# Flow attention in a decoder kernel: token totals and inverses laid out as 128 rows by 128 columns, spread by row tiles in plain fp32 into a ring of five banks

## The reference, cut to what matters

```python
qkv = x @ qkv_w.T + qkv_b                       # q, k, v per head
q = jax.nn.sigmoid(q); k = jax.nn.sigmoid(k)
k_sum = k.sum(axis=2)
sink_incoming = 1.0 / jnp.sum((q + EPS) * (k_sum[:, :, None, :] + EPS), axis=-1)
q_sum = q.sum(axis=2)
source_outgoing = 1.0 / jnp.sum((k + EPS) * (q_sum[:, :, None, :] + EPS), axis=-1)
k_so_sum = (k * source_outgoing[..., None]).sum(axis=2, keepdims=True)
conserved_sink = jnp.sum((q + EPS) * (k_so_sum + EPS), axis=-1) + EPS
q_si_sum = (q * sink_incoming[..., None]).sum(axis=2, keepdims=True)
conserved_source = jnp.clip(jnp.sum((k + EPS) * (q_si_sum + EPS), axis=-1) + EPS, -1.0, 1.0)
sink_allocation = jax.nn.sigmoid(conserved_sink)
source_competition = jax.nn.softmax(conserved_source, axis=-1) * float(n)
kv = jnp.einsum('bhnd,bhnm->bhdm', k, v * source_competition[..., None])
out = jnp.einsum('bhnd,bhdm->bhnm', q * sink_incoming[..., None], kv) * sink_allocation[..., None]
out = out.transpose(0, 2, 1, 3).reshape(b, n, c) @ proj_w.T + proj_b
```

## Time and profile before

| what | value |
| --- | --- |
| device time, three runs | 2602.89, 2605.04, 2608.36 us (median 2605.04) |
| the profiled execution: its time | 2608.17 us |
| its span, first to last instruction | 2606.3 us |
| busy share of the span | PE 90%, PEld 50%, DVE 61%, ACT 48%, POOL 27% |
| mean granted TensorE clock | 0.979 of full speed |
| chain that ended last, by engine | PE 61%, DVE 18%, ACT 14%, issue 4%, POOL 2% |

### The profile page before, as it was taken

The page is one execution under the profiler, slowest core; times in us unless marked ns, Lnnn a source line. Parts: engine busy times, 40 slices in busy tenths (PEclk is TensorE's granted clock), DMA queues, the critical chain, the costliest instruction groups (busy, mean ns, idle before and its releaser), DMA issues.

```text
span 2606.3 us, 37060 instructions
## 1 busy us (share of the span) xinstructions
PE 2350.9 (90%) x13000; PEld 1303.8 (50%) x13000; DVE 1591.2 (61%) x3101; ACT 1247.5 (48%) x2870; POOL 691.7 (27%) x989
## 2 busy tenths in 40 slices
PE   7989999989988999998898999999899899999866
PEld 3655544545565544454556554435455655444443
DVE  4664643569866462457977655155797746516698
ACT  5763212259675321227967431222886723122396
POOL 0002140037401232013820213201480031310366
PEclk9999999999999999999999999999999999999988
DMA  8001010010210200001030101001003010100000
GB/s 300 18 11 49 24 45 33 0 49 1 87 50 10 72 29 17 32 1 49 9 128 2 55 26 29 32 17 49 1 9 128 2 58 23 29 17 1 0 1 33
DMA packets 58988, 99.43 MB, mean 38 GB/s; under 512 B 13364, under 2 KB 13748, under 8 KB 58296
## 3 DMA queue, kind: packets, MB, share of 16 engines
q1 hardware_dynamic: 58808, 97.06, 11.3%
HBM read 88.66 MB, written 8.39 MB: 37 GB/s over the span
## 4 chain that ended last, share of the span: by engine, by line
PE 61%; DVE 18%; ACT 14%; issue 4%; POOL 2%; DMA 0%; ACTq 0%; DVEq 0%; POOLq 0%; SPq 0%
PE psum L398 20%; PE psum L392 13%; ACT prob L810 6%; PE psum L424 4%; PE psum L483 3%; DVE neg_max L1106 3%; PE psum L549 2%; DVE f_a L1113 2%; PE psum L451 2%; PE psum L791 2%; DVE bn L1056 2%; DVE f_top L1392 2%; PE psum L620 1%; ACT f_z L1008 1%; PE psum L763 1%
## 5 line engine op out<-in xcount | busy, mean ns | idle before, releaser
L398 PE MATMUL psum<-weights,mixed 128*128 128x512 f32 x768 | 341.2, 595 | 0.0
L392 PE MATMUL psum<-xT,weights 128*128 128x512 f32 x768 | 334.5, 593 | 0.0
L810 ACT ACTIVATE prob<-psum,neg_max 128x128 f32<-128x128 f32 (+3 forms) x512 | 265.0, 543 | 109.3 <-DVE neg_max L1106 109.3
L1430 POOL TENSOR_SCALAR var<-stats 128x1 f32<-128x1 f32 x192 | 63.8, 332 | 797.2 <-DVE stats L1057 797.1
L1106 DVE TENSOR_REDUCE neg_max<-psum 128x1 f32<-128x128 f32 (+3 forms) x512 | 217.5, 483 | 81.2 <-PE psum L488 46.5
L846 ACT COPY xT<-psum 128x512 f32<-128x512 f32 x128 | 70.3, 590 | 367.4 <-PE psum L451 367.4
L1087 DVE TENSOR_TENSOR x<-psum,x 128x512 f32<-128x512 f32 x128 | 88.4, 691 | 244.8 <-PE psum L398 172.7
L398 PE MATMUL psum<-weights,xT 128*128 128x512 f32 x512 | 232.9, 598 | 2.4 <-DVE recip L1295 1.6
L1443 POOL TENSOR_TENSOR f_a<-f_a,f_z 128x256 f32<-128x256 f32 x256 | 204.5, 809 | 113.8 <-DVE f_a L1113 113.8
L392 PEld LDWEIGHTS psum<-xT,weights 128*128 128x128 f32 x768 | 144.0, 190 | 172.4 <-issue 172.2
L398 PEld LDWEIGHTS psum<-weights,mixed 128*128 128x128 f32 x768 | 141.6, 190 | 167.5 <-issue 166.7
(11 more groups left out here) (246 smaller groups left out, 4193.1 us busy)
## 6 DMA issues: line engine op xcount, KB each, us to landing
xT<-in_xT SPq DMA_DIRECT2D x8, 1024.0 KB, 6.4
x<-in_x SPq DMA_DIRECT2D x8, 1024.0 KB, 8.9
out<-x SPq DMA_DIRECT2D x16, 512.0 KB, 2.8
weights<-in_a_k SPq DMA_DIRECT2D x4, 1024.0 KB, 5.3
weights<-in_a_q SPq DMA_DIRECT2D x4, 1024.0 KB, 5.1
weights<-in_a_v SPq DMA_DIRECT2D x4, 1024.0 KB, 5.0
w1f<-in_w SPq DMA_DIRECT2D x4, 1024.0 KB, 14.9
w2f<-in_w SPq DMA_DIRECT2D x4, 1024.0 KB, 17.3
```

Of the source, the lines that this page charges most:

```text
L392: last = mm(bank[:, 0:n], weights[weight][:, c, heads(g)], rhs(c), start=(c == 0), stop=(c == C - 1))
L398: last = mm(bank, lhsT(c), weights[weight][:, c, :], start=(c == 0), stop=(stop and c == C - 1))
L810: last = run(sb["prob"][:, slot, o:o + keys], bank[:, o:o + keys], ACT.Exp, bias=sb["neg_max"][:, n, qc, j:j + 1], accum_out=sb["a_sum"][: ...
```

## The change

Stage D's per-token numbers are laid out otherwise. A window of 512 tokens is cut in four quarters of 128. Where one bank held 32 rows per chunk (each head's value in eight equal rows) by 512 tokens, it now holds for each head a row (pair) per quarter, by 128 tokens: `d_quarters` issues 16 matmuls of 128 columns, which accumulate over the quarters `c` with weights that are zero outside the quarter's rows (`quarters`). VectorE's add and reciprocal then work on 128 x 128. `d_spread` takes each chunk's 32 rows as a row tile of the array and issues 16 plain fp32 matmuls of 32 rows to 128 columns, 128 tokens wide, into four banks at once; ScalarE's and GpSimd's split into halves goes away, and so do `d_coarse`, `d_halves` and `d_sel_r`. `dve_ring` is widened by banks 6 and 7 from the first `d_sums` to the first `d_out`. `d_source` is one step for both windows (256 columns), `d_weigh` one transpose per window in place of four. The constants are split in four `d_sums` steps with a `d_weights` step of VectorE ahead of each, and the order of the list is new: the weights from q's sums, `d_sums` and `d_total 1` stand among the last projections of k, `d_spread 1` ahead of the last of them, and the sinks stand behind `d_weigh 1`.

```diff
+OF_K, OF_Q, OF_SOURCE, OF_SINK = range(4)
+SUM_ORDER = [OF_Q, OF_K, OF_SINK, OF_SOURCE]
+TOTAL_ORDER = [1, 3, 0, 2]
+    def widen(self, banks):
+        n = len(self.names)
+        k = (n - self.first) % len(self.banks)
+        self.banks, self.first = banks + self.banks[k:] + self.banks[:k], n
+    def narrow(self, pe, banks):
+        self.drained(pe)
+        self.banks = banks
...
+    steps += [("d_weights", OF_Q), ("d_project", 1, 1, 0), ("d_sums", OF_Q), ("d_total", 1), ("d_project", 1, 1, 1), ("d_project", 1, 1, 2),
+              ("d_spread", 1), ("d_project", 1, 1, 3), ("d_table",)]
...
+    steps += [("d_turn", 0), ("d_turn", 1), ("d_total", 3), ("d_weights", OF_K), ("d_value", 0), ("d_sums", OF_K), ("d_total", 0), ("d_spread", 3),
+              ("d_value", 1), ("d_total", 2), ("d_spread", 0), ("d_weights", OF_SINK), ("d_value", 2), ("d_turn", 2), ("d_spread", 2),
+              ("d_value", 3), ("d_sums", OF_SINK), ("d_weights", OF_SOURCE), ("d_value", 4), ("d_turn", 3),
+              ("d_sums", OF_SOURCE), ("d_source",), ("d_value", 5), ("d_turn", 4), ("d_turn", 5), ("d_value", 6), ("d_weigh", 0), ("d_turn", 6),
+              ("d_turn", 7), ("d_value", 7), ("d_weigh", 1)] + [("d_sink", 0, g) for g in range(C)] + [("d_kv",)]
...
-            def d_compact(bank, i, src, w):
-                for g in range(C):
-                    last = mm(bank[HD * g:HD * g + HD, :], sb["d_thin"][:, i, g, :], src[:, g, tokens(w)],
-                              start=True, stop=True)
-                last.then_inc(dve_ring.filled, 1)
+            def d_quarters(bank, i, src, w):
+                for c in range(WT):
+                    for g in range(C):
+                        last = mm(bank[HD * g:HD * g + HD, :], sb["d_thin"][:, i, c, g, :], src[:, g, w * D + P * c:w * D + P * c + P],
+                                  start=(c == 0), stop=(c == WT - 1))
+                return last
...
                 elif kind == "d_spread":
-                    pe.wait_ge(q["d_halves_ready"], at("d_halves_ready", n + 2))
-                    for g in range(C):
-                        mm(dve_ring.claim(pe, ("d_spread", n, g)), sb["d_sel_r"][:, g, :], sb["d_halves"][:, n % 2, :],
-                           start=True, stop=True).then_inc(dve_ring.filled, 1)
+                    pe.wait_ge(q["d_inverse_ready"], at("d_inverse_ready", TOTAL_ORDER.index(n) + 1))
+                    spread = [dve_ring.claim(pe, ("d_spread", n, g)) for g in range(C)]
+                    for c in range(WT):
+                        for g, bank in enumerate(spread):
+                            r = slice(HD * g, HD * g + HD)
+                            last = mm(bank[:, heads(c)], sb["d_sel"][r, c, :], sb["d_inv"][r, n, :], start=True, stop=True)
+                            if c == WT - 1:
+                                last.then_inc(dve_ring.filled, 1)
+                elif kind == "d_source":
                     bank = dve_ring.claim(pe, step)
+                    for w in range(W):
+                        last = d_quarters(bank[:, heads(w)], OF_SOURCE, sb["d_kT"], w)
...
-            def eps_weights(sums, out, blocks):
+            def eps_weights(i, sums, out, pattern):
+                of_chunk = sb["d_tot"][:, i, :]
+                link(v.scalar_tensor_tensor(of_chunk, sums[:, 0, :], FLOW_EPS, sums[:, 1, :], ALU.add, ALU.add))
+                each = of_chunk[:, :, None].broadcast_to([P, C, P]) if i == OF_SINK else \
+                    of_chunk[:, None, :, None].broadcast_to([P, WT, C, HD])
+                v.tensor_tensor(out, pattern, each, ALU.mult).then_inc(q["d_weights_ready"], 1)
```

More of the change, by code:

```diff
@@ L662, in _ @@
                     bank = dve_ring.claim(pe, step)
-                    for g in range(C):
-                        mm(bank[HD * g:HD * g + HD, 8:10], sb["d_thin"][:, 2, g, :], sb["flow_eps"][:], start=True, stop=True)
-                    for g in range(C):
-                        last = mm(bank[:, 2 * g:2 * g + 2], sb["d_blk"][:, C + g, :], sb["flow_eps"][:], start=True, stop=True)
+                    for w in range(W):
+                        last = d_quarters(bank[:, heads(w)], OF_SOURCE, sb["d_kT"], w)
@@ L667, in _ @@
                     last.then_inc(dve_ring.filled, 1)
-                elif kind == "d_source":
-                    d_compact(dve_ring.claim(pe, step), 2, sb["d_kT"], arg[0])
                 elif kind == "d_weigh":
                     w, = arg
-                    pe.wait_ge(q["d_e_ready"], at("d_e_ready", w + 1))
-                    bank = dve_ring.claim(pe, step)
-                    for t in range(WT):
-                        last = nc.tensor.transpose(bank[:, heads(t)], sb["d_inv"][:, W + w, heads(t)], ident[:])
-                    last.then_inc(dve_ring.filled, 1)
+                    pe.wait_ge(q["d_e_ready"], at("d_e_ready", 1))
@@ L678, in _ @@
+                    nc.tensor.transpose(dve_ring.claim(pe, step)[:, 0:P], sb["d_e"][:, heads(w)], ident[:]).then_inc(dve_ring.filled, 1)
                 elif kind == "d_kv":
                     taken(pe, ("d_turn", T - 1))
-                    bank = dve_ring.claim(pe, ("d_esum",))
-                    for g in range(C):
-                        last = mm(bank[:, 2 * g:2 * g + 2], sb["d_sel"][:, g, :], sb["d_esum"][:], start=True, stop=True)
-                    last.then_inc(dve_ring.filled, 1)
+                    pe.wait_ge(q["d_shares_ready"], at("d_shares_ready", 1))
@@ L706, in _ @@
                     w, t = divmod(arg[0], WT)
+                    if w + t == 0:
+                        dve_ring.narrow(pe, banks[3:6])
                     taken(pe, ("d_fold", C - 1))
@@ L1323, in _ @@
+                        v.tensor_tensor(vt, vt, e, ALU.mult).then_inc(dve_ring.freed if t == WT - 1 else q["d_v_weighed"], 1)
                 elif kind == "d_kv":
-                    bank = dve_ring.take(dve, ("d_esum",))[:, 0:2 * C].rearrange("p (g w) -> p g w", w=W)
-                    v.tensor_reduce(sb["d_fac"][:], bank, AX.X, ALU.add).then_inc(dve_ring.freed, 1)
+                    bank = dve_ring.take(dve, ("d_esum",))
+                    v.reciprocal(sb["d_fac"][:], bank[:, 0:C]).then_inc(dve_ring.freed, 1)
@@ L1624, in place @@
     put("blocks", [P])
-    put("odd_rows", [1])
+    put("quarters", [WT, HD])
     put("stacked", [SK])
```

174 lines of the change are left out of this document (80 added, 94 removed).

## The result

The changed kernel takes 2559.97 us (median of 4 runs, 2558.67 to 2560.47) against 2606.35 us for the kernel before (4 runs, 2602.89 to 2608.36): a ratio of 0.9823, 95% interval 0.9806 to 0.984, 46.4 us less on the medians. The profiled execution took 2559.72 us with a span of 2557.9, where before it was 2608.17 and 2606.3: 48.4 us less.

What follows compares the result with a forecast made beforehand. TensorE, busy 90% of the span, was taken as the bound; 46.0 us content plus 0.5 us waits per entry gave 52.7 us less, 2555.5 us, and 3.1 us to the median made 2552 us, range 2539 to 2576.

Steps and rivals of the forecast that it cites:

- TensorE's content: Stage D's steps to the first `d_kv` matmul, added up by kind without waits: 46.0 us per batch entry.
- the halves of the source: Two halves of `d_source` in stage D, each priced like a total from stage A's records: 1.01 us each.
- `d_weigh` with the sum of exponentials: Stage D: two transposes for `d_weigh`, 0.3 us, and one 128-column load with a narrow matmul, 0.3 us.
- Waits: TensorE's waits in stage D, mostly covered by VectorE, narrowly at three places: 0.5 us per entry in all.
- The loads: A spread's 32 weight loads in stage D: about 1.1 us, still fitting; bounds for the whole 2545 and 2566 us.
- the stage A row: Stage A's 16 loads of 32 x 128 within 0.54 us, 0.03 each, taken to decide the spreads' load time.
- the series rival: Row tiles' loads pass one after another: 3.9 us a spread in stage D, 2597 us in all; chance 0.08.
- The gain: Stretch from last k projection to `d_kv`: 14.2 us less in the first entry, 12.8 in each other, 52.7 total.
- I let it stay up: Clock in stage D's stretch: no fall, since no stand is near the 1.44 us after which it fell.
- From the profile to the median: Whole kernel: the median of the runs lies 3.1 us below the profiled execution, so 2555.5 becomes 2552 us.
- The slower rival: Each spread record in stage D waits for its own load: 7.4 us a spread, 2653 us; chance 0.03.
- the hidden-gain rival: Work behind `d_kv` waits on something of its own, so an earlier start is lost; chance 0.02 with no change.

Runs made afterwards that it cites:

- the banks and the turns' order alone: Kernel before with a five-bank ring in stage D and turns 0 to 3 ahead of the first constants: 2584.28 us, ratio 0.9915.
- the seams: Changed kernel with turns moved to make six more borders between tiled and full-size groups: 2552.70 us, one execution only.
- the two filled gates: Changed kernel with stage C's third base tile ahead of the first gate, 2538.81 us; then also the sixth ahead of the fifth output tile, 2539.15 us.
- the first filled gate: Changed kernel with only stage C's third base tile moved ahead of the first gate: 2538.81 us, ratio 0.9749 to the kernel before.
- the banks alone: Kernel before with the ring of five banks in stage D and nothing else of the change: 2594.27 us, ratio 0.9949.

## Why the prediction was right, and where it was off

The forecast was 2552 us, 2539 to 2576. The mechanism held; three sizes were off: the stretches by 1.9 us, the clock elsewhere by 2.4, the step from the profile to the median by 3.4, which with 0.4 of rounding are the 8.0 us.

- **TensorE's content.** 46.0 us an entry, 46.97 measured. The terms by kind were right: spread 1.10 for 1.09, total 0.99 to 1.02 for 1.01, value tile 3.43. Two were a little high: the halves of the source 1.86 for 2.02, and `d_weigh` with the sum of exponentials 0.36 for 0.6. What was missing is a term: the seams. The stretch has 14 borders between tiled and full-size groups, and at 0.09 us they are 1.3 us, 5 us over the program. This 0.09 is only what shows on the full-size groups. Each half of the source behind the first costs 1.86 - 0.99 = 0.87 us, so some 0.12 of a total's 0.99 belongs to the change of tiles behind it; that is why the halves, counted as two whole totals, were too high. A total pays it straight ahead of a spread as well. It could have been read: in the earlier trace rows eight transposes between two tiled groups take 78.81 - 77.79 = 1.02 us, where the earlier trace rows gives 2 x 0.44 = 0.88 for as many among full-size ones. The Trainium skill (TensorEngine Tiling (Array Packing), "Key Properties") says that changing the tiling mode drains TensorE; the runs agree in that each change costs time, 0.09 us on the full-size group beside it.
- **Waits.** 0.5 us an entry forecast, none measured. The claim that five banks and the narrow inverse cover it "narrowly" is shown from both sides: one bank less costs 4.47 us an entry, as the same walk gave (4.5), and the old inverse's time 4.2.
- **The loads.** The step that went by the stage A row was right. What the series rival feared is real when row tiles are absent (3.57 us a spread) or stand in the wrong order (2.75), and absent in the order used (1.10). By the rule of the Trainium skill on LDWEIGHTS, cited in the prediction, 3.4 us: near the 3.57 of the full array, while for row tiles the page's other rule, that they overlap, is what the runs show.
- **The gain.** 52.7 us forecast, 50.8 in the stretches. Its split by cause was loose: I put 4.8 us an entry on the spreads without saying what of it needs new tiles. With the banks and the turns' order alone, the stretch falls from 102.4 to 96.0.
- **The clock.** In stage D right: no fall in 20 stretches (four in each of the two profiles of the changed kernel, of the seams and of the two filled gates). "I let it stay up" was thought out for this stretch alone. Elsewhere the falls behind unchanged stands came or stayed away in pieces of 1.7 us. In the first profile there were two pieces more of them than before, 3.4 us, and the span gained 2.4 us less than the stretches.
- **From the profile to the median.** I carried over that the median lies 3.1 us under the profiled execution. After, it lies 0.25 above. With the fourth execution of the kernel before, whose median is 2606.35, it would have been 1.8. The likeliest source is again the number of half-clock pieces of one execution: the kernel before ran between 2602.9 and 2608.4 us, three such pieces, and the changed kernel's 2556.78 us had a mean clock of 0.982 where 2559.6 to 2560.5 had 0.980.

The slower rival and the hidden-gain rival had nothing for them in any run. What stays open: what decides whether a stand is followed by half clock. The stand of 1.44 us had it in some entries of three kernels and in none of a fourth; the 2.50 us stand of stage B had it in four and three entries of the changed kernel's two profiles, and in one of the first filled gate's. The Trainium skill (TensorE: Matmul & The Clock Gate, "Part 1: The HAM clock gate") says that how much runs at the lower clock varies from run to run with the gate's phase; the two profiles of the changed kernel agree, by 3.4 us, but no run here set the phase.

## What to carry to other kernels

Before new tiles are written for a stage, try what the list and the idle banks give: here they were 21 of 46 us, and at full clock the banks alone gave nearly all of that. Count the seams between tiled and full-size matmuls (0.09 us each), issue row tiles in turn and never one after the other, and ask of a narrower operation whether it is its own time or the engine that waits for it that pays. And compare two kernels by the stretch at full clock: executions of one kernel lay up to 8.5 us apart here, and the two profiles of the changed kernel differed by 3 us with 3.4 us of half clock between them.

## What the runs showed of the hardware that was not expected

- Sixteen fp32 matmuls of 32 rows in four row tiles take 1.10 us in turn and 2.75 one tile after the other, with the same records; the same columns on the full array take 3.57. One tile after the other, a tile still starts while the one before has three of its eight records to go.
- The stand that was filled in stage C has its cause in VectorE, beside GpSimd. Four small products of `c_gm` take 3.79 us at the first gate, where GpSimd's additions run; at the second gate, when it is idle, the same four take 0.63:

```profile
333.83 3.79 DVE L1265 TENSOR_TENSOR c_gm<-c_gate,c_mid 128x64 f32<-128x64 bf16 x4
...
347.41 0.63 DVE L1265 TENSOR_TENSOR c_gm<-c_gate,c_mid 128x64 f32<-128x64 bf16 x4
```

```profile
327.37 10.04 POOL L1475 TENSOR_TENSOR x<-x,c_bias_o 128x512 f32<-128x512 f32 x8
```

  The Trainium skill (Trainium Architecture — The Big Picture, "What this means for kernel authors") says that VectorE and GpSimd share a port and lock each other out. The rows agree: the first three products take 1.22 to 1.30 us each, as long as one of the eight additions (10.04 / 8 = 1.26), and the fourth, which starts at 337.42 us, just as the additions end (327.37 + 10.04 = 337.41), takes 0.21. No run here moved the additions, so the cause is argued, not shown.
